# Routing of the 32-expert stage in four chunks of tokens, moved into the block of the token scatters

## The reference

```python
x = layernorm(x + _L1_attn_ref(x, ...))
x = layernorm(x + _L1_xattn_ref(x, ctx_768, ...))
x = layernorm(x + _L1_ffn_ref(x, gate_w, w_gate_up, w_down,
                              shared_w_gate_up, shared_w_down))   # E=32, K=4, H=256, I=128, C=256
x = layernorm(x + _L2_attn_ref(x, ...))
x = layernorm(x + _L2_xattn_ref(x, ctx, ...))    # "bitnet": ternary weights, int8 activations
...
```

## Time and profile before

| | us |
|---|---|
| median of 3 runs (lowest, highest) | 2917.51 (2912.9, 2920.44) |
| the profiled execution | 2911.88 |
| its span, first to last instruction | 2910.0 |
| routing block, about | 1074 to 1117 |
| scatter block, about | 1117 to 1216 |
| expert block begins (its first DMA issue) | 1215.99 |

### The profile page before, as it was taken

How to read it: one execution, slowest core, us unless ns; L and a number is a source line. 1 busy time by engine, 2 the same in 40 slices (tenths; PEclk the granted TensorE clock), 3 DMA queues, 4 the chain that set the end, 5 groups by cost and what they waited for, 6 DMA issues and landing times. The chain is left out here.

```text
span 2910.0 us, 36903 instructions
## 1 busy us (share of the span) xinstructions
PE 2197.5 (76%) x13274; PEld 1453.7 (50%) x13281; DVE 1706.5 (59%) x4376; ACT 934.1 (32%) x1687; POOL 819.9 (28%) x776
## 2 busy tenths in 40 slices
PE   6888689967887774385678676677777776697886
PEld 3544378834553542273345343566666665435332
DVE  3753310056744748244485576768888886527496
ACT  0142222220251231132205464334444444315343
POOL 1001200032001004552100001777777777203000
PEclk9999589989998886697889898889898898798898
DMA  8200244419006223474500202522222222100000
GB/s 224 69 21 2 69 152 180 177 54 227 20 23 134 87 104 129 166 226 173 113 4 22 80 1 87 119 54 58 54 53 55 55 62 51 41 31 1 0 0 29
DMA packets 128187, 233.74 MB, mean 80 GB/s; under 512 B 38985, under 2 KB 76745, under 8 KB 124049
## 3 DMA queue, kind: packets, MB, share of 16 engines
q1 hardware_dynamic: 68768, 122.49, 14.5%
q0 software_dynamic: 51952, 100.65, 11.5%
q10 hardware_dynamic: 7296, 8.40, 1.0%
HBM read 247.17 MB, written 66.72 MB: 108 GB/s over the span
## 5 line engine op out<-in xcount | busy, mean ns | idle before, releaser
L2962 POOL DMA_INDIRECT L2f_G<-in_L2f_table,L2f_idx x512 | 532.2, 1039 | 175.2 <-issue 151.2
L3284 DVE CUSTOM_DVE_ANT_0 L2f_junk<-L2f_G,L2f_X 128x256 bf16<-128x256 f32 x512 | 182.8, 421 | 135.2 <-DMA L2f_G<-in_L2f_table,L2f_idx 134.9
L3019 PE MATMUL psum<-L2f_G,L2f_diag 128*128 128x256 f32 x768 | 184.9, 393 | 0.0
L3019 PEld LDWEIGHTS psum<-L2f_G,L2f_diag 128*128 128x128 f32 x768 | 152.5, 200 | 22.3
L1181 PE MATMUL psum<-constb 128*128 128x256 bf16 x512 | 92.5, 287 | 72.1 <-PEq L983 38.3
L2996 PE MATMUL psum<-xT,L2f_mw 128*128 128x256 f32 x512 | 135.1, 412 | 13.7 <-DVE L2f_h L3290 13.6
L2418 POOL DMA_INDIRECT picks_x<-L1f_rows,L1f_put x64 | 70.7, 1105 | 239.1 <-ACT L1f_rows L2508 220.2
L3150 ACT ACTIVATE L2f_diag<-const,L2f_actd 128x128 f32<-128x128 f32 x400 | 123.9, 388 | 30.1 <-DVE L2f_actd L3298 30.1
L2996 PEld LDWEIGHTS psum<-xT,L2f_mw 128*128 128x128 f32 x512 | 107.8, 213 | 34.0 <-DVE L2f_h L3290 15.7
L3143 ACT ACTIVATE L2f_actd<-L2f_dots 128x9 f32<-128x9 f32 (+1 forms) x64 | 13.5, 210 | 302.5 <-DVE L2f_dots L3284 302.5
L3006 PE MATMUL psum<-L2f_h,L2f_mw 128*128 128x256 f32 x256 | 75.1, 421 | 45.2 <-DVE L2f_acc L3334 45.2
(11 more groups left out here) (663 smaller groups left out, 5032.1 us busy)
## 6 DMA issues: line engine op xcount, KB each, us to landing
L1f_we<-in_L1f_w SPq DMA_DIRECT2D x32, 384.0 KB, 8.5
picks_x<-zeros SPq DMA_DIRECT2D x16, 544.0 KB, 7.9
L1f_xe<-picks_x SPq DMA_DIRECT2D x32, 272.0 KB, 2.9
picks_y<-zeros SPq DMA_DIRECT2D x16, 512.0 KB, 6.4
L2f_G<-in_L2f_table,L2f_idx POOLq DMA_INDIRECT x512, 2.8
slots_x<-zeros POOLq DMA_DIRECT2D x8, 512.0 KB, 7.8
L1f_wb<-in_L2x_w SPq DMA_DIRECT2D x1, 4096.0 KB, 12.1
L1f_g<-picks_y SPq DMA_DIRECT2D x8, 512.0 KB, 12.2
```

The costliest lines, as they stand in the source:

```text
L2962: nc.gpsimd.indirect_dma_start(out=G[:, h, k, :], out_offset=None, in_=ins["L2f_table"], in_offset=bass.IndirectOffsetOnAxis(ap=IDX[:, t, ...
L3019: mm = nc.tensor.matmul(ps[:, MIX + t % 2, 0:D], diag[:, i % 2, k, :], row[:, D:2 * D], start=(h == 0 and k == 0), stop=(h == HEADS - 1 an ...
L3284: e = VE.tensor_tensor_reduce(out=junk[:, k, :], in0=row[:, 0:D], in1=X[:, t % 3, :], scale=1.0, scalar=0.0, op0=ALU.mult, op1=ALU.add, ac ...
```

## The change

The routing block is gone. Its work stands in the scatter block, ahead of what was there on each engine, and is cut into NCH = 4 chunks of SET = 4 tiles:

- PE: logits of chunk 0, transposes of chunk 0, then for each further chunk its logits, the places of the chunk before, its transposes; last the places of chunk 3.
- VectorE: `route(n)` for the four chunks, one after another, then the block's old work. Within a chunk the four one-hots are one instruction, the four products one and the four reductions one. `Mc` has one more column that is carried to the next chunk. Four small writes to `rows` that need no routing stand ahead of chunk 0.
- ScalarE: an Exp ahead of each chunk's four row copies.
- GpSimd: waits for `routed` once a chunk. The scatters are the same 64.
- SP: the same loads, now the first in this block.
- `lg`, `M`, `oh` and `pos` lie in `acc`, which the shared expert writes later; `down(0)` waits for `routed` for that reason.

```diff
-            with nc.Block() as block:
...
                 @block.gpsimd
                     for t in range(NT):
+                        if t % SET == 0:
+                            pool.wait_ge(s["routed"].sem, s["routed"].at(t // SET + 1))
                         pool.wait_ge(s["row_ready"].sem, s["row_ready"].at(t + 1))
...
+                    logits(0)
+                    turn(0)
+                    for n in range(1, NCH):
+                        logits(n)
+                        places(n - 1)
+                        turn(n)
+                    places(NCH - 1)
                     up(0)
...
                     for t in range(NT):
+                        if t % SET == 0:
+                            n = t // SET
+                            act.wait_ge(s["route_dve"].sem, s["route_dve"].at(2 * n + 1))
+                            nc.scalar.activation(lg[:, t:t + SET, :], lg[:, t:t + SET, :], ACT.Exp).then_inc(s["route_act"].sem, 1)
                         act.wait_ge(s["turned"].sem, s["turned"].at(t + 1))
...
+                    def route(n):
...
+                        link(V.tensor_tensor(oh[:, :, :, :], iota,
+                                             ef[:, tiles, :].rearrange("p t k -> p k t").unsqueeze(3).broadcast_to([P, K, SET, E]),
+                                             ALU.is_equal))
+                        link(V.tensor_tensor(pos[:, 0:2, :, :], oh[:, 0:2, :, :], oh[:, 2:4, :, :], ALU.add))
+                        link(V.tensor_tensor(M[:, tiles, :], pos[:, 0, :, :], pos[:, 1, :, :], ALU.add))
+                        if n:
+                            link(V.tensor_copy(Mc[:, 0, :], Mc[:, SET, :]))
+                        for t in range(SET):
+                            link(V.tensor_tensor(Mc[:, t + 1, :], Mc[:, t, :], M[:, n * SET + t, :], ALU.add))
...
+                        dve.wait_ge(s["placed"].sem, s["placed"].at(n + 1))
+                        link(V.tensor_tensor(pos[:, :, :, :], ps[:, 4 + n, 0:SET * E].rearrange("p (t e) -> p t e", e=E)
+                                             .unsqueeze(1).broadcast_to([P, K, SET, E]), oh[:, :, :, :], ALU.mult))
+                        link(V.tensor_reduce(pk[:, tiles, :].rearrange("p t k -> p k t"), pos[:, :, :, :], AX.X, ALU.add))
...
+                        link(V.tensor_tensor(put[:, tiles, :], f, none[:, tiles, :], ALU.add))
+                        V.memset(sm[:, tiles], 0.0).then_inc(s["routed"].sem, 1)
+                    for n in range(NCH):
+                        route(n)
                     nc.vector.tensor_reduce(mxs[:, 0:1], c.cT[:, :, :], AX.XY, ALU.max, apply_absolute_value=True)\
                         .then_inc(s["bit_max"].sem, 1)
```

More of the change, by code:

```diff
@@ L2297, in moe_top4_stage @@
         with ExitStack() as part:
-            lg = sb("lg", [P, NT, E], F32, part)
+            sg = sb("sg", [P, 2, CH], F32, part)
+            qw = sb("qw", [P, BITNET_N], BF16, part)
+            SET = NT // NCH
+            room = lambda j, a: acc[:, j, a * NT * E:(a + 1) * NT * E]
+            lg, M = (room(1, a).rearrange("p (t e) -> p t e", e=E) for a in range(2))
+            oh, pos = (room(0, a).rearrange("p (k t e) -> p k t e", k=K, e=E) for a in range(2))
             mx, sm = sb("mx", [P, NT], F32, part), sb("sm", [P, NT], F32, part)
@@ L2302, in moe_top4_stage @@
             ef = sb("ef", [P, NT, K], F32, part)
[L2303 to L2306, removed]
+            Mc = sb("Mc", [P, SET + 1, E], F32, part)
+            Mb, Mcb = sb("Mb", [P, SET, E], BF16, part), sb("Mcb", [P, SET, E], BF16, part)
             pk, ok = sb("pk", [P, NT, K], F32, part), sb("ok", [P, NT, K], F32, part)
@@ L2424, in _ @@
                 def _(sp):
+                    sp.dma_start(wb[:, :], ins["L2x_w"]).then_inc(s["even_landed"].sem, 16)
+                    sp.dma_start(bias[:, :], ins["w_L2x"]).then_inc(s["even_landed"].sem, 16)
+                    c.prefetch(sp, name)
+                    for e in range(NW):
+                        sp.dma_start(we[:, e, :], ins["L1f_w"][e]).then_inc(s["w_first"].sem, 16)
                     sp.wait_ge(s["bit_q"].sem, s["bit_q"].at(3))
@@ L2433, in _, with logits, turn, places @@
                 def _(pe):
[L2434 to L2437, removed]
-                            mm = nc.tensor.transpose(ps[:, t % 2, j * P:(j + 1) * P], c.xT[:, j, t * P:(t + 1) * P], c.ident)
-                        mm.then_inc(s["turned"].sem, 1)
+                    c.wait_weights(pe, name)
+                    def logits(n):
+                        for t in range(n * SET, (n + 1) * SET):
+                            for j in range(DH):
+                                mm = nc.tensor.matmul(ps[:, 4 + n, (t % SET) * E:(t % SET + 1) * E], c.xT[:, j, t * P:(t + 1) * P],
+                                                      w["gate"][:, j * E:(j + 1) * E], start=(j == 0), stop=(j == DH - 1))
+                        mm.then_inc(s["route_pe"].sem, 1)
+                    def turn(n):
+                        for t in range(n * SET, (n + 1) * SET):
+                            if t >= 2:
+                                pe.wait_ge(s["row_ready"].sem, s["row_ready"].at(t - 1))
+                            for j in range(DH):
+                                mm = nc.tensor.transpose(ps[:, t % 2, j * P:(j + 1) * P], c.xT[:, j, t * P:(t + 1) * P], c.ident)
+                            mm.then_inc(s["turned"].sem, 1)
+                    def places(n):
+                        pe.wait_ge(s["route_dve"].sem, s["route_dve"].at(2 * n + 2))
+                        flat = lambda x: x[:, :, :].rearrange("p t e -> p (t e)")
+                        nc.tensor.matmul(ps[:, 4 + n, 0:SET * E], c.before, flat(Mb), start=True, stop=False)
+                        nc.tensor.matmul(ps[:, 4 + n, 0:SET * E], c.ones, flat(Mcb), start=False, stop=True)\
+                            .then_inc(s["placed"].sem, 1)
                     def up(n):
@@ L2540, in _ @@
                 def _(dve):
+                    V = nc.vector
+                    link = Chain(dve, s["dve_chain"])
+                    c.wait_weights(dve, name)
+                    iota = w["iota"].unsqueeze(1).unsqueeze(1).broadcast_to([P, K, SET, E])
+                    none = w["spare"].rearrange("p (t k) -> p t k", k=K)
+                    V.memset(rows[:, :, D:D + 1], 0.0)
+                    V.tensor_scalar(rows[:, :, D + 9:D + 13], none, float(-SLOTS - 4 * T), None, ALU.add)
+                    V.memset(rows[:, :, D + 13:ROW], 0.0)
@@ new lines, in _ @@
+                    link(V.memset(Mc[:, 0, :], 0.0))
+                    def route(n):
+                        tiles = slice(n * SET, (n + 1) * SET)
+                        wide = lambda m: m.unsqueeze(2).broadcast_to([P, SET, E])
+                        l = lg[:, tiles, :]
+                        dve.wait_ge(s["route_pe"].sem, s["route_pe"].at(n + 1))
+                        link(V.tensor_copy(l, ps[:, 4 + n, 0:SET * E].rearrange("p (t e) -> p t e", e=E)))
+                        link(V.tensor_reduce(mx[:, tiles], l, AX.X, ALU.max))
+                        V.tensor_tensor(l, l, wide(mx[:, tiles]), ALU.subtract).then_inc(s["route_dve"].sem, 1)
+                        dve.wait_ge(s["route_act"].sem, s["route_act"].at(n + 1))
+                        link(V.tensor_reduce(sm[:, tiles], l, AX.X, ALU.add))
+                        link(V.reciprocal(sm[:, tiles], sm[:, tiles]))
+                        link(V.tensor_tensor(l, l, wide(sm[:, tiles]), ALU.mult))
+                        for t in range(n * SET, (n + 1) * SET):
+                            e = V.max(m8[:, t, :], lg[:, t, :])
+                        link(e)
+                        for t in range(n * SET, (n + 1) * SET):
+                            e = V.max_index(i8[:, t, :], m8[:, t, :], lg[:, t, :])
+                        link(e)
+                        link(V.tensor_copy(ef[:, tiles, :], i8[:, tiles, 0:K]))
+                        link(V.tensor_tensor(oh[:, :, :, :], iota,
[7 more added lines that the diff above has]
+                            link(V.tensor_tensor(Mc[:, t + 1, :], Mc[:, t, :], M[:, n * SET + t, :], ALU.add))
+                        link(V.tensor_copy(Mb[:, :, :], M[:, tiles, :]))
+                        V.tensor_copy(Mcb[:, :, :], Mc[:, 0:SET, :]).then_inc(s["route_dve"].sem, 1)
+                        link(V.tensor_reduce(mx[:, tiles], m8[:, tiles, 0:K], AX.X, ALU.add))
+                        link(V.reciprocal(mx[:, tiles], mx[:, tiles]))
+                        V.tensor_copy(rows[:, tiles, D + 1:D + 5], ef[:, tiles, :])
+                        V.tensor_tensor(rows[:, tiles, D + 5:D + 9], m8[:, tiles, 0:K],
+                                        mx[:, tiles].unsqueeze(2).broadcast_to([P, SET, K]), ALU.mult)
+                        dve.wait_ge(s["placed"].sem, s["placed"].at(n + 1))
+                        link(V.tensor_tensor(pos[:, :, :, :], ps[:, 4 + n, 0:SET * E].rearrange("p (t e) -> p t e", e=E)
```

(12 more changed lines are left out.)

4 lines of the change are left out of this document (2 added, 2 removed).

## The result

The changed kernel takes 2891.26 us (median of 4 runs, 2889.88 to 2895.52) against 2917.4 us before (4 runs, 2912.9 to 2920.44). The ratio is 0.9921, 95% interval 0.9904 to 0.9938: 23 us less, between 18 and 28. The forecast was 2892.2, in a range of 2884 to 2903.

What follows compares the result with a forecast made beforehand. Logits, routing and 64 scatters were taken to bound the block. Scatters beside routing let the bit_kv store end it at 1190.7 instead of 1215.99, a 25.3 us gain: 2917.5 - 25.3 = 2892.2 us, range 2884 to 2903.

Steps and rivals of the forecast that it cites:

- What bound the kernel: Scatter block's end: one chain of logits, routing and 64 scatters sets it; only GpSimd is late for 27 us.
- the rival that would have undone it: Stage: gain comes from merged block or shorter instructions, not overlap; stage under 130 us, total under 2906; no chance given.
- First scatter: GpSimd in the merged block: scatters start at 1088.8, 30.1 us earlier, after chunk 0's logits and routing.
- the prices by size: VectorE's routing: instruction times by element count give 10.1 us a chunk, 9.9 for the first.
- PE's order: PE in routing: placing places(n) behind logits(n+1) costs VectorE nothing; otherwise 1 us a chunk.
- first rival: Chunks 1 to 3: routing instructions hold scatters up to 13.2 us, 1.5 taken; time 2900.6, chance 0.18 whole or part.
- second rival: Chunks 1 to 3: 60 VectorE instructions wait 0.97 us each for scatters; time 2950, chance 0.03; 1.2 us taken.
- the row: Earlier trace, VectorE beside scatters: a 7-element instruction at 1131.03 took 0.37 us against 0.17 for the same width.
- third rival: Early scatters: loads fill the DMA engines and GpSimd stands until about 1104; time 2902.8, chance 0.08.
- What is late next: Block's end: bit_kv issued 1.5 us later, its store lands at 1190.2, after GpSimd's 1187.4, and ends the block.
- The total: Whole program: 25.3 us gain from the median 2917.5, giving 2892.2 us.

## Why the prediction was right, step by step

- **What bound the kernel.** Right, and the rival that would have undone it was run: without the overlap the gain is gone. The 27 us in which only GpSimd was late are SP's wait of 27.1.
- **First scatter.** Forecast 30.1 us earlier; it was 30.3 (44.4 to 14.15). The chunks took 9.56, 10.03, 9.82 and 10.07 us (starts of L2508 at 1083.39, 1092.95, 1102.98 and 1112.80, end 1122.87) against 9.9 and 10.1 from sizes and slopes. With no scatter beside them they took 9.57 and 9.77, so the prices by size were 0.3 us a chunk too high. Since a four-dimensional instruction over 512 elements took 0.69 us like a flat one, nothing was lost in the bulk forms.
- **PE's order** cost nothing with chunks of 4: VectorE has no wait for `placed` in the changed kernel's list. It begins to cost with larger chunks (12.2 us of PE in a chunk of 8).
- **Scatters held by the routing** (first rival, 0 to 13.2 us, 1.5 taken). The size was too large. Of the scatters beside the routing two were held:

```profile
1107.91 1.07 POOL L2335 DMA_INDIRECT picks_x<-L1f_rows,L1f_put  x1 [0.30 <-issue]
...
1116.95 1.24 POOL L2335 DMA_INDIRECT picks_x<-L1f_rows,L1f_put  x1 [0.30 <-issue]
...
1148.60 4.96 POOL L2335 DMA_INDIRECT picks_x<-L1f_rows,L1f_put  x1 [0.31 <-issue]
```

  0.10 and 0.27 us over the 0.97 of the others, 0.4 in all; the last row is the one beside the 4096-wide instruction, as in the earlier trace rows. By the rule of the Trainium skill (SBUF — State Buffer, Who interferes with whom) a VectorE instruction with two SBUF inputs and a GpSimd instruction that reads SBUF contend, and the one issued first blocks the other for its whole length. The trace agrees for the long instruction (4.96 us) and not for those of 0.7 us and less: 21 of the 23 scatters that started beside the routing kept their 0.97 to 1.01 us.
- **VectorE held by the scatters** (second rival, 1.2 us taken): 0.6 us. The three chunks that ran beside scatters took 10.03, 9.82 and 10.07 us, and 9.77 each in the run in which the scatters wait for all chunks. The difference lies in a few short instructions, as with the row; one cast of 16 elements took 0.37 us in place of 0.17. VectorE's old work began 43.18 us after the stage's first matmul in the changed kernel and 42.58 in that run.
- **The loads** (third rival). Scatters started 1.27 us apart while the DMA engines were 0.91 busy; only their landing took longer (for the 20 of the first window 5.6 us in the median and 6.4 at most, against a median of 2.5 over all 64). GpSimd did not wait for it.
- **What is late next.** Right in kind: the store, and 2 us ahead of it GpSimd. Wrong in size: `bit_kv` was to be issued 1.5 us later than before, and came at 107.6 against 107.7. Of the terms, the later start of the old work was 0.05 us (42.58 without scatters beside the routing, against 42.53 before) and not 1.25, the scatters' hold on VectorE 0.6 and not 1.2, and VectorE's wait for PE behind the sums fell from 1.54 to 0.75 us, nearly as forecast. By these `bit_kv` came 1.6 us earlier than forecast. The store landed after 6.1 us and not 6.5, and the expert block's first DMA came 0.4 us behind it, not 0.5. Together these make the stage's gain 27.4 us instead of 25.3. What the prediction left out, 0 to 1.5 us won in the expert block after the shorter pause of PE, did not show: the expert block's first eight matmuls took 1.97 us, and 1.94 before.
- **The total.** The medians differ by 26.1 us, the ratio says 23 (18 to 28). The interval holds both the 25.3 forecast and the 27.4 of the stage; the runs cannot tell these apart. That 2892.2 lies within 1 us of the measured median is luck: the interval is 10 us wide, and the terms were off by 2 us in one direction.

## What to carry to other kernels

Where one engine sends a long train of equal steps (64 scatters, 1.28 us each) that needs only a part of what the engine ahead of it computes, cut that computation so that the first piece is done early and each further piece takes less time than the train's share: 10 us of routing for 20 us of scatters kept GpSimd busy from its first scatter on.

Then find the second chain before estimating the gain: here the wait at the block's end (27.1 us) was what could be won as long as the second chain stayed as it was. After the change 6.5 us added to VectorE's routing moved the end of the block by 6.3, while leaving out half of the scatters moved it by 0.2.

Smaller pieces cost the chain that makes them (40 us in four chunks, 31 in two), larger ones the chain that waits for them (first scatter at 14.2 against 24.3 us); uneven pieces, the first one small, gave the shortest stage of those tried (110.6 us).

## What was not expected of the hardware

In these traces a scatter that ran beside many short VectorE instructions was almost never held, though one 4096-wide instruction held one for 4 us: 0.4 us in all beside 30 us of routing, against 4.0 us for the one long instruction. The other way round the scatters cost that routing 0.6 us.

Where GpSimd ended the block, the time from the last scatter's end to the next block was 7.2 to 7.3 us when no store was under way beside it, and 7.9 and 8.7 us in the two profiles where a 1 MB store started beside the last scatters. The last scatter landed 2.5 to 2.6, 3.2 and 4.0 us after its start, so from that landing to the next block it is 5.6 to 5.7 us each time, while the next block began 0.4 us after the landing of the last store. What fills these 5.6 us no run shows.
